# A one-core graph and expert network: weights loaded a stage ahead, a bias as one bf16 product split by GpSimd, later root waits, stage ends without GpSimd's drain

## The reference, cut to what matters

```python
x = x + gnn(ln(x))     # agg = segment_sum(ew * x[dst], src); h = (1 + eps) * x + agg;
                       # twice: h = relu(batchnorm(h @ W + b))
x = x + moe(ln(x))     # 8 experts, top 2: gelu(xe @ W1 + b1) @ W2 + b2, weighted by the router
x = x + hconv(ln(x))   # twice: h = relu(h @ w1 + b1); agg = segment_sum(ew * h[src], dst);
                       #        h = relu(bn(agg @ w2 + b2)), then bn, relu
x = x + gated(ln(x))   # shared 3-layer MLP + 4 small expert MLPs, top 2 of a softmax gate
```

## Time and profile before

| | |
|---|---|
| median of 3 runs | 5671.06 us (5665.08 to 5693.91) |
| the profiled execution: its own time | 5663.62 us |
| its span, first to last instruction | 5661.9 us |
| mean granted TensorE clock | 0.833 of full |
| busy share of the span | PE 69%, DVE 36%, ACT 34%, POOL 52% |
| scattered_sum, both segment_sums | about 1532, 1016 and 1020 us |
| expert_ffn, gated_mlp | about 810 and 339 us |
| combine_message | about 127 us (2769.3 to 2896.0) |

### The profile page before, as it was taken

The page is one execution under the profiler, slowest core; times in us unless marked ns, Lnnn a source line. Parts: engine busy times, 40 slices in busy tenths (PEclk is TensorE's granted clock), DMA queues, the critical chain, the costliest instruction groups (busy, mean ns, idle before and its releaser), DMA issues. The chain is left out here.

```text
span 5661.9 us, 84772 instructions
## 1 busy us (share of the span) xinstructions
PE 3894.2 (69%) x19824; PEld 3291.2 (58%) x19825; DVE 2028.0 (36%) x5367; ACT 1935.5 (34%) x4772; POOL 2966.6 (52%) x2583
## 2 busy tenths in 40 slices
PE   2666666666667599999765566667466556664898
PEld 1555555555565488888555556566456556663665
DVE  5444444455446511111332222233422222226333
ACT  2222222223234222222243333333633333336422
POOL 2888888888810022222037777774277777760000
PEclk9777778888886699999888778898777887886699
DMA  6766766767740255555323333332233333320000
GB/s 225 89 87 88 88 88 88 87 87 88 83 154 0 97 198 176 194 176 191 140 86 102 102 102 102 102 103 61 82 102 103 102 102 102 101 84 0 16 20 19
DMA packets 353878, 568.90 MB, mean 100 GB/s; under 512 B 61597, under 2 KB 274459, under 8 KB 350992
## 3 DMA queue, kind: packets, MB, share of 16 engines
q0 software_dynamic: 198720, 337.81, 30.2%
q1 hardware_dynamic: 150820, 226.00, 12.3%
q10 hardware_dynamic: 4268, 4.30, 0.3%
HBM read 404.84 MB, written 163.07 MB: 100 GB/s over the span
## 5 line engine op out<-in xcount | busy, mean ns | idle before, releaser
L638 POOL DMA_INDIRECT A<-h_rows,segment_sum_idx x1568 | 1537.4, 980 | 772.5 <-issue 399.6
L675 PE MATMUL bank<-A 128*128 128x128 f32 x7808 | 1247.4, 331 | 795.3 <-PEq L69 795.3
L675 PEld LDWEIGHTS bank<-A 128*128 128x128 f32 x7808 | 1182.8, 242 | 860.1 <-issue 858.4
L392 POOL DMA_INDIRECT node_sums<-T,scattered_sum_idx x784 | 1215.6, 1550 | 350.5 <-issue 225.3
L654 ACT ACTIVATE A<-A,segment_sum_edge 128x256 f32<-128x256 f32 x1568 | 667.9, 496 | 1171.7 <-DMA A<-h_rows,segment_sum_idx 1171.7
L463 PE MATMUL bank<-X,T 128*128 x1952 | 631.9, 481 | 94.8 <-PEq L69 92.3
L457 PE MATMUL bank<-T 128*128 128x128 f32 x1952 | 350.8, 336 | 425.8 <-PEq L69 425.7
L703 DVE TENSOR_TENSOR T<-T,bank 128x256 f32 x488 | 205.2, 420 | 1105.8 <-DVEq L69 1101.2
L463 PEld LDWEIGHTS bank<-X,T 128*128 128x128 f32 x1952 | 463.2, 249 | 191.9 <-issue 115.0
L457 PEld LDWEIGHTS bank<-T 128*128 128x128 f32 x1952 | 309.7, 239 | 438.9 <-issue 433.9
L498 DVE SCALAR_TENSOR_TENSOR T<-T,edges,not_after 128x128 f32<-128x128 int16 x784 | 223.7, 347 | 553.6 <-DVEq L69 511.0
(11 more groups left out here) (281 smaller groups left out, 4521.8 us busy)
## 6 DMA issues: line engine op xcount, KB each, us to landing
T<-in_L_ffn_W SPq DMA_DIRECT2D x52, 1024.0 KB
A<-in_L_ffn_W SPq DMA_DIRECT2D x52, 1024.0 KB, 8.5
T<-src_lanes SPq DMA_DIRECT2D x196, 128.0 KB, 3.4
A<-h_rows,segment_sum_idx POOLq DMA_INDIRECT x1568, 2.8
node_sums<-A SPq DMA_DIRECT2D x3, 6528.0 KB, 33.5
A<-node_sums SPq DMA_DIRECT2D x36, 512.0 KB, 5.5
h_rows<-A SPq DMA_DIRECT2D x50, 256.0 KB, 2.1
node_sums<-T,scattered_sum_idx POOLq DMA_INDIRECT x784, 4.1
```

The source lines that it names most:

```text
L392: pool.indirect_dma_start(c.sum_dram[at % COPIES], bass.IndirectOffsetOnAxis(ap=idx[:, h % LR, j:j + 1], axis=0), msg[:, h % LR * G + j, : ...
L638: pool.indirect_dma_start(msg[:, h * G + j, :], None, c.h_dram, bass.IndirectOffsetOnAxis(ap=idx[:, h, j:j + 1], axis=0)).then_inc(landed[ ...
L675: mm = pe.matmul(acc[s][:, k * P:(k + 1) * P], msg[:, h * G + j, k * P:(k + 1) * P], hot[:, s, j, :], start=(j == 0), stop=(j == G - 1))
```

## The change

Four edits. (1) Two permanent weight buffers `c.w[0]`, `c.w[1]` take the weights of the product stages and of combine_message in turn; SP issues each load in a stage ahead (`load_w`), and the stage's own load and buffer go. (2) In combine_message the two float32 bias products per block become one bf16 product of a 128x128 matrix of ones with `pieces` (128x512), written over the whole bank before the four weight products. `pieces` holds the bias split in three bf16 parts on rows 0, 32 and 64, zero elsewhere; GpSimd makes it in a body that it did not have before, from a bias that is now broadcast to 128 rows. (3) `finish_stats` is cut in two, `begin_stats` up to the hand-over to ACT and `finish_roots` from the wait for the root; in combine_message the second half of parts 1, 2 and 3 stands after the first pass of the next part. (4) Every stage's block is opened with `no_gpsimd_drain=True`: GpSimd's DRAIN of L94 is not in the program, its DRAIN of L96 still is.

```diff
-        with nc.Block() as block:
+        with nc.Block(no_gpsimd_drain=True) as block:
...
+def load_w(eng, c, slot, w_dram):
+
+    eng.dma_start(c.w[slot][:], w_dram.rearrange("(k p) n -> p k n", p=P)).then_inc(c.w_in[slot], 16)
...
+            load_w(sp, c, 0, a["L0_gnn_W1"])
+            load_w(sp, c, 1, a["L0_gnn_W2"])
             for name, (at, rows) in c.pat.items():
...
     dve.tensor_scalar(rstd, var, EPS, None, ALU.add).then_inc(act_go, 1)
+
+
+def finish_roots(dve, act_done, c, v, at):
+
+    rstd = c.rstd[:, at]
     take(dve, act_done)
     chain(dve, dve.reciprocal(rstd, rstd), v)
-    chain(dve, dve.scalar_tensor_tensor(c.shift[:, at], mean, -1.0, rstd, ALU.mult, ALU.mult), v)
+    chain(dve, dve.scalar_tensor_tensor(c.shift[:, at], c.mean[:, at], -1.0, rstd, ALU.mult, ALU.mult), v)
+
+
+def finish_stats(dve, act_go, act_done, c, v, at=slice(0, NB)):
+
+    begin_stats(dve, act_go, c, v, at)
+    finish_roots(dve, act_done, c, v, at)
...
+        @block.sync
+        def _(sp):
+            load_w(sp, c, next_slot, next_w)
...
-def norm_product(nc, c, w_dram, bias, gamma, beta):
+def norm_product(nc, c, w, w_ready, bias, gamma, beta):
...
-        @block.sync
-        def _(sp):
-            sp.dma_start(w[:], w_dram.rearrange("(k p) n -> p k n", p=P)).then_inc(w_in, 16)
-            sp.wait_ge(w_in, 16)
...
-            pe.wait_ge(w_in, 16)
+            pe.wait_ge(*w_ready)
             blocks(pe, product)
...
+            load_w(sp, c, 0, a["L1_gnn_c1_w1"])
+            load_w(sp, c, 1, a["L1_gnn_c1_w2"])
             with sp.Fori(1, last_step(sp) + 1) as q:
...
-def combine_message(nc, c, w_dram, b_dram):
+def combine_message(nc, c, w, w_ready, b_dram):
 
     PARTS = ((0, 6), (6, 16), (16, 26), (26, 38), (38, 50))
     WIDE = 12
 
     def run(block, sb, sem):
-        w, bias, one = sb("w", [P, KD, D]), sb("bias", [1, D]), sb("one", [1, P])
+        bias, one = sb("bias", [P, D]), sb("one", [P, P], BF16)
+        pieces, left, third, part = sb("pieces", [P, 2, D], BF16), sb("left", [P, D]), sb("third", [P, D], BF16), sb("part", [P, D])
+        mask = sb("mask", [P, 3])
         y = [carve(flat(c.T), r * 2 * WIDE * D, (2, WIDE * D)) for r in range(2)]
         col = [sb(f"col{s}", [P, KD, BLK]) for s in range(2)]
         row = [sb(f"row{s}", [P, 2, D]) for s in range(2)]
         turn, out = c.ps[0:2], c.ps[2:4]
-        w_in, b_in, v, go, done, stored, h_out = (sem(n) for n in ("w_in", "b_in", "v", "go", "done", "stored", "h_out"))
+        b_in, v, go, done, stored, h_out = (sem(n) for n in ("b_in", "v", "go", "done", "stored", "h_out"))
         y_in, y_free, stats_ready = pair(sem, "y_in"), pair(sem, "y_free"), [sem(f"stats_ready{n}") for n in range(len(PARTS))]
         row_ready, turned, col_ready, row_free, col_free = (pair(sem, n) for n in ("row_ready", "turned", "col_ready", "row_free", "col_free"))
         prod, out_free, one_made = pair(sem, "prod"), pair(sem, "out_free"), sem("one_made")
+        made = sem("made")
 
         @block.sync
         def _(sp):
@@ -1740,9 +1752,8 @@
                     sp.dma_start(y[n % 2][:, k, 0:(hi - lo) * D], rows[:, lo * D:hi * D]).then_inc(y_in[n % 2], 16)
 
             load(0)
-            sp.dma_start(w[:], w_dram.rearrange("(k p) n -> p k n", p=P)).then_inc(w_in, 16)
-            sp.dma_start(bias[:], b_dram[None, :]).then_inc(b_in, 16)
             load(1)
+            sp.dma_start(bias[:], b_dram[None, :].to_broadcast([P, D])).then_inc(b_in, 16)
             for n in range(2, len(PARTS)):
                 take(sp, y_free[n % 2])
                 load(n)
@@ -1751,6 +1762,30 @@
                 sp.dma_start(c.h_dram[j * BLK:(j + 1) * BLK, :].rearrange("(t p) d -> p t d", p=P),
                              c.A[:, j * 2:j * 2 + 2, :]).then_inc(h_out, 16)
             sp.wait_ge(h_out, 16 * NJ)
+
+        @block.gpsimd
+        def _(pool):
+            tt, ts = pool.tensor_tensor, pool.tensor_scalar
+            for n in range(3):
+                ts(mask[:, n:n + 1], c.node[:, 0:1], float(n * 32), None, ALU.is_equal).then_inc(made, 1)
+            pool.memset(one[:], 1.0).then_inc(made, 1)
+            take(pool, made, 4)
+            pool.wait_ge(b_in, 16)
+
+            chain(pool, pool.tensor_copy(third[:], bias[:]), made)
+            tt(left[:], bias[:], third[:], ALU.subtract).then_inc(made, 1)
+            ts(part[:], third[:], mask[:, 0:1], None, ALU.mult).then_inc(made, 1)
+            take(pool, made, 2)
+            chain(pool, pool.tensor_copy(third[:], left[:]), made)
+            tt(left[:], left[:], third[:], ALU.subtract).then_inc(made, 1)
+            ts(bias[:], third[:], mask[:, 1:2], None, ALU.mult).then_inc(made, 1)
+            take(pool, made, 2)
+            tt(part[:], part[:], bias[:], ALU.add).then_inc(made, 1)
+            ts(left[:], left[:], mask[:, 2:3], None, ALU.mult).then_inc(made, 1)
+            take(pool, made, 2)
+            chain(pool, tt(part[:], part[:], left[:], ALU.add), made)
+            for q in range(2):
+                pool.tensor_copy(pieces[:, q, :], part[:]).then_inc(one_made, 1)
 
         @block.scalar
         def _(act):
@@ -1801,16 +1836,15 @@
                 take(pe, col_ready[s])
                 if j >= 2:
                     take(pe, out_free[s])
+                pe.matmul(out[s][:], one[:], pieces[:].rearrange("p t d -> p (t d)"), start=True, stop=False, skip_group_check=True)
                 for q in range(2):
-                    at = out[s][:, q * D:(q + 1) * D]
-                    pe.matmul(at, one[:], bias[:], start=True, stop=False)
                     for k in range(KD):
-                        mm = pe.matmul(at, col[s][:, k, q * P:(q + 1) * P], w[:, k, :], start=False, stop=(k == KD - 1))
+                        mm = pe.matmul(out[s][:, q * D:(q + 1) * D], col[s][:, k, q * P:(q + 1) * P], w[:, k, :],
+                                       start=False, stop=(k == KD - 1), skip_group_check=True)
                 mm.then_inc(prod[s], 1)
 
-            pe.wait_ge(w_in, 16)
-            pe.wait_ge(b_in, 16)
-            pe.wait_ge(one_made, 1)
+            pe.wait_ge(*w_ready)
+            pe.wait_ge(one_made, 2)
             turn_rows(0)
             for j in range(NJ):
                 if j + 1 < NJ:
@@ -1819,7 +1853,11 @@
 
         @block.vector
         def _(dve):
-            dve.memset(one[:], 1.0).then_inc(one_made, 1)
+            def close(n):
+                lo, hi = PARTS[n]
+                finish_roots(dve, done, c, v, slice(lo, hi))
+                dve.sem_inc(stats_ready[n], 1)
+
             for n, (lo, hi) in enumerate(PARTS):
                 r = n % 2
                 take(dve, y_in[r], 32)
@@ -1828,13 +1866,16 @@
                         ins = dve.scalar_tensor_tensor(c.X[:, t, :], y[r][:, k, (t - lo) * D:(t - lo + 1) * D], c.pick[:, t, k:k + 1],
                                                        c.X[:, t, :], ALU.mult, ALU.add)
                     chain(dve, ins, v)
+                    if k == 0 and n >= 2:
+                        close(n - 1)
                 dve.sem_inc(y_free[r], 1)
                 for t in range(lo, hi):
                     stat_tile(dve, c, t)
                 dve.drain().then_inc(v, 1)
                 take(dve, v)
-                finish_stats(dve, go, done, c, v, slice(lo, hi))
-                dve.sem_inc(stats_ready[n], 1)
+                begin_stats(dve, go, c, v, slice(lo, hi))
+                if n == 0 or n == len(PARTS) - 1:
+                    close(n)
...
+        c.w = [sb(f"w{i}", [P, KD, D]) for i in range(2)]
+        c.w_in = [nc.alloc_semaphore(f"w_in{i}") for i in range(2)]
...
-        combine_message(nc, c, a["L1_gnn_c1_w1"], a["L1_gnn_c1_b1"])
-        segment_sum(nc, c, c.edges, SRC, DST, c.dst_ranges)
-        aggregate_product(nc, c, a["L1_gnn_c1_w2"], col("L1_gnn_c1_b2"), col("L1_gnn_c1_g"), col("L1_gnn_c1_b"))
+        combine_message(nc, c, c.w[0], (c.w_in[0], 32), a["L1_gnn_c1_b1"])
+        segment_sum(nc, c, c.edges, SRC, DST, c.dst_ranges, 0, a["L1_gnn_c2_w1"])
+        aggregate_product(nc, c, c.w[1], (c.w_in[1], 32), col("L1_gnn_c1_b2"), col("L1_gnn_c1_g"), col("L1_gnn_c1_b"))
```

More of the change, by code:

```diff
@@ L828, in root_affine, with summed_product @@
     act.sqrt(c.affine[:, 0, :], c.affine[:, 0, :]).then_inc(done, 1)
-def summed_product(nc, c, w_dram, bias, gamma, beta):
+def summed_product(nc, c, w, w_ready, bias, gamma, beta):
     CH = 2
@@ L837, in run @@
     def run(block, sb, sem):
-        w, row = sb("w", [P, KD, D]), [sb(f"row{s}", [P, 2, D]) for s in range(2)]
+        row = [sb(f"row{s}", [P, 2, D]) for s in range(2)]
         stats, agg = sb("stats", [P, KD, NJ, 6]), sb("agg", [P, KD, 2])
```

45 lines of the change are left out of this document (18 added, 27 removed).

## The result

The changed kernel takes 5640.29 us (median of 7 runs, 5634.96 to 5648.98), before takes 5675.26 us (7 runs, 5665.08 to 5693.91). The ratio is **0.9935**, with a 95% interval of 0.9918 to 0.9952: 37 us or 0.65% faster, between 27 and 47. That lies in the predicted range (5637 to 5670), but nearer to the rival "no price" (5639) than to the likeliest case (5652.8).

The account below looks back on a forecast made before the run. No engine was busy throughout; 18 stages stand behind one another, with PE bounding combine_message. Terms -11 (combine_message), -7.6 (weights) and +0.4 (scattered_sum), DRAINs 0, sum to -18.2: 5652.8 us, range 5637 to 5670.

Parts of the forecast that it names:

- no price: Stage ends: L96's remaining DRAIN doesn't wait for the DMA work, so 13.35 us more is won, 5639; 14%.
- the likeliest case: Whole kernel: DRAIN costs on the path unchanged, the other terms as summed, -18.2 us, 5652.8; 38%.
- the first rival: Stage ends: DRAIN's own price after any indirect DMA; three hidden ends each pay 4.5 us anew at L96, 5666; 33%.
- the second rival: Stage ends: the remaining DRAIN at L96 doesn't wait for this at all, 13.35 us more won, 5639; 14%.
- reading one: Stage ends: L94's DRAIN is the end of GpSimd's indirect DMA work; L96 pays 4.47 and 8.88 at two ends, gain 0.
- The price is the DRAIN's own: Stage ends: price due after any indirect DMA; prepare and two segment_sums pay 4.5 us each at L96, +13.5, 5666; 33%.
- The DRAIN of L94 goes, but the one of L96 stays: Stage ends: the first DRAIN is removed, the one behind the rendezvous remains; in the likeliest case gain 0.
- 3.81 - 1.34 + 0.31 = 2.78: combine_message, PE block at full clock: 3.81 us less bias pairs, plus one bf16 product, gives 2.78 us (2.69 to 3.09).
- This wait goes: combine_message: DVE's wait of 3.92 us for ACT's root, behind PE's blocks in ACT's order, disappears.
- the cautious part of it: Product stages' starts: clock may rise no earlier, giving 4.6 of 9.2 us; four fifths taken, 7.3.
- the removed waits of 9.2: Starts of norm_product, aggregate_product (twice) and message_rows: waits between input and first product, 1.7, 2.6 twice and 2.3 us.
- 0: combine_message: GpSimd's split of 4 to 8 us is hidden, since PE would only wait for stats_ready(1) later.

Follow-up runs that it names:

- e8: The changed kernel with one plain GpSimd DRAIN put back in every stage end, behind the rendezvous and ahead of L96's: ratio 0.9980 to before.
- e6: Before with only the two float32 bias products per block contracted over 128 rows instead of one: ratio 0.9961 to before, combine_message 114.33 us.
- e7: The changed kernel with its bf16 bias product contracted over row 0 alone: ratio 0.9947 to before, combine_message 115.30 us.
- e2: Before with only the weights loaded a stage ahead; DRAINs, bias products and root waits as before: ratio 0.9995 to before, combine_message 144.65 us.
- e3: Before with weights loaded ahead, the bf16 bias product and GpSimd's split; root waits and DRAINs as before: ratio 0.9958 to before, combine_message 109.61 us.
- e5: The changed kernel with the root waits back at the end of their own part: ratio 0.9940 to before, combine_message 109.29 us.
- e10: The changed kernel without deferred root waits, PE's wait for the split bias behind the first two blocks' transposes: ratio 0.9941 to before, combine_message 109.49 us.

## Why the prediction came out as it did

**The DRAINs: the likeliest case was wrong, the first rival right in its premise and wrong in its end, the second rival right in its time.** The prediction's reading one was that the DRAIN is "the end of GpSimd's work on its indirect DMAs", to be paid at L96 at two ends. e8 refutes the first half for the indirect DMAs: the price is due at any later time, as the rival "The price is the DRAIN's own" had it, with 4.47 and 3.98 as its sizes at scattered_sum and the segment_sums; in prepare, where that rival wanted 4.5 us too, it is 0.39. Both failed at the step "The DRAIN of L94 goes, but the one of L96 stays", where I took the two for the same instruction: the likeliest case then put "4.47 and 8.88 as before, gain 0" at L96, and the runs show 0.163 and 0.107 there. The one in L96 belongs to the clearing of the semaphores, and neither it nor the one of L97 behind it pays. So 4.47 + 8.88 = 13.35 us are won, the figure of the rival that had 14 in 100. That L96's DRAINs had "stood behind a first one" was a fair doubt, and only a run could lift it. The Trainium skill's rule ("Perfetto Trace Analysis", "Sequencer-only Instruction (DRAIN, etc)"), that the profile shows such an instruction without its semaphore wait, agrees with e8: the plain DRAIN behind scattered_sum's rendezvous, where no engine is awaited any more, takes 4.469 us.

**The range held by the no-price rival, and in part by luck.** The likeliest case forecast a gain of 18.2 us, and 35 to 37 came. The prediction gave 17 in 100 to a time over 0.5% below before's, which is what came. The range's lower end was low enough only because it took in the no-price case. That this case's 5639 was met to 1 us is chance too: it is a gain of 31.6 counted from 5671.06, the median of three runs, where seven have 5675.26.

**combine_message: -15.0 instead of -11, outside the bounds by 1.** The schedule was right to a few tenths. Counted from the stage's start, as 2769.3 before and 2762.3 after, stats_ready(1), (2) and (3) were forecast at 2807.5, 2823.7 and 2841.8 and came at 2808.2, 2824.1 and 2841.6. Too dear was the block: "3.81 - 1.34 + 0.31 = 2.78" against 2.38. The bf16 product took 0.22 and not 0.31, the lower bound (the Trainium skill's 215.7 ns, quoted in the prediction, agrees); and taking the one-row products away frees 0.3 us more than the 1.34, because, as e6 and e7 show, each change between one row and 128 rows had cost PE some time at both of its sides. The Trainium skill, "TensorEngine Tiling (Array Packing)", section "Key Properties", says that a change of tiling mode drains TensorE. e6, where 3.81 became 3.03 with the same products, would fit that, but no run shows whether a product over one row is such a change, or the drain itself.

What the prediction didn't have at all is the clock. It took before's 16 us at 0.50 as PE's start-up, due in any kernel. All but some 5 of them, which the changed kernel has too, belonged to the one-row products: 17, 24 and 37 us of unbroken work in three executions, none over 8 in any kernel without them. The stage thus gains 15 us against the execution that was profiled, and 18 to 32 against the other two. Why one-row products keep the granted clock low when PE is busy without a gap stays open: e7 shows that one of them per block, in bf16, doesn't, and since it changes the type and the number at once, no run tells which of the two matters. The whole fits an old stage that is often longer than the one profiled: the bias edit is worth some 23 us between e2 and e3, and e6 24, by their middle values more than the 15 of the one pair of profiles.

**The deferral was costed right and judged rightly for part 1 (4 us later), but its gain was put on the wrong edit.** "This wait goes" (3.92 us) was credited to it; e5 shows 0.47 without it. It costs 3.1 to 3.7 us of the stage. The stage with the bias edit alone is 109.3 to 109.6.

**The weights: -8.0 in the profiled execution, -7.6 forecast.** Over the profiles of ten kernels with the loads ahead (all but e8, whose stages hold its DRAIN) and three without, the four stages are shorter by 0.8, 3.9, 3.8 and 2.2 us in the mean, 10.6 in all, 0.9 beyond the bound of 9.7. The term was some 3 us too small; the cautious part of it, that the clock might rise no sooner, wasn't called for. What the gain over the removed waits of 9.2 comes from stays open, and the whole of e2, 3 us faster than before (between 10 faster and 4 slower), doesn't confirm the size. The loads ahead in scattered_sum (+0.4 forecast) don't show in 1521 to 1537.

**GpSimd's split** took 8.9 us (2775.07 to 2783.94 in the first two rows below, POOL's timeline), a little over the 4 to 8 forecast, and `pieces` was late: PE's first work stands 21.7 us behind the stage's start and not 19.7. "0" held, since e10 gets the 2 us back and gains nothing. What it costs DVE: the 20 multiply-adds of part 1, 8.24 us in the earlier trace rows's pattern, are 9.02 beside it, in the last row (DVE's timeline of the changed kernel):

```profile
2775.07 0.40 POOL L1775 CAST combine_message_third<-combine_message_bias 128x256 bf16<-128x256 f32 x1 [12.00 <-DMA combine_message_bias<-in_L_gnn_c_b]
...
2783.00 0.94 POOL L1788 CAST combine_message_pieces<-combine_message_part 128x256 bf16<-128x256 f32 x2 [0.17 <-POOLq L69]
...
2781.36 9.02 DVE L1866 SCALAR_TENSOR_TENSOR X<-T,pick,X 128x256 f32<-128x256 f32 x20 [0.36 <-DVEq L69]
```

That is 0.8 us. The Trainium skill's rule ("SBUF — State Buffer", "SBUF: two separate sides") was priced at 4 to 8. The trace agrees that the two get in each other's way: three of the multiply-adds during the split took 0.61 to 0.95 us instead of 0.48. But only the last 2.6 of the split's 8.9 us lay beside multiply-adds.

**The sum.** Forecast -18.2: -11, -7.6, +0.4 and 0. Measured in one pair of executions: -15.0, -8.0, nothing that shows, and -13.4 for the DRAINs, -36.4 together; the pair of spans has 23.6, since scattered_sum, the first segment_sum and gated_mlp happened to be 3.7 + 4.5 (the DRAIN that isn't there), 3.3 and 2.0 us longer, and the rest sums to 0.7 us less. The medians of seven runs, where such scatter averages out, have 35, the ratio 37.

## What to carry to other kernels

Before an edit takes an instruction out, look at whether what stays behind is the same instruction: here GpSimd's plain DRAIN costs 4 to 9 us once behind indirect DMAs, and the one that goes with the clearing of semaphores at most 0.17 there. A product that contracts over one row (a bias added by ones) is dear in two ways that its own duration doesn't show: the products around it take longer, and the granted clock may stay low for tens of us; the same product over 128 rows of ones/128 is faster with no other change. Two edits on one wait don't add: measure the deferral without the edit that makes it needless.

## What the runs showed of the hardware that was not expected

- GpSimd's first plain DRAIN behind indirect DMAs: 4.47 to 4.52 us behind scattered_sum's scatter-adds, 8.88 behind expert_ffn's gathers and scatters, 3.97 and 3.98 behind a segment_sum's gathers, even when it comes over 20 us after GpSimd's last gather. A second one right behind: 0.040 us. The one at the clearing of the semaphores, with none before it: 0.06 to 0.25 us over all stages. In prepare, with no indirect DMA: 7.69 us at once, 0.39 some 40 us later.
- PE busy for 17, 24 and some 37 us on end at the granted clock 0.50 (1.2 GHz) with float32 one-row products among its work; with 128-row products in their place 0.67 on average in the first 8 us.
- A float32 bias pair of 256 columns at full clock: 0.62 us over one row, 0.44 over 128 rows. A bf16 product of 512 columns: 0.32 over one row, 0.22 over 128, from its start to the next one's.
